# First loop of a two-layer kernel: the causal mask moves from TensorE's score matmuls to an affine select by GpSimd on the exponentials

## The chip, the core and the metric

The kernel runs on one core of a Trainium2 chip. A core has a matmul engine (TensorE, "PE" in the rows, with its weight loads as "PEld"), VectorE ("DVE"), ScalarE ("ACT"), GpSimd ("POOL") and SyncE ("SP", which issues most DMAs here). Each engine works through its own list of instructions in order; they meet through semaphores only. The metric is the device time of one execution in microseconds (us); lower is better.

## The reference, cut to what matters

There are two layers on a batch of 8 sequences of 512 tokens with 128 features. Layer 0 adds an attention block and a mixture-of-experts block to its input; layer 1 adds a gated delta-rule block and a second mixture of experts. The change touches layer 0's attention only (16 heads of 8 features, rotary positions, keys and values from a normalised latent of 32):

```python
scores = jnp.einsum('bhqd,bhkd->bhqk', q, k) / jnp.sqrt(jnp.float32(HEAD_DIM))
causal = jnp.tril(jnp.ones((t, t), dtype=bool))
scores = jnp.where(causal[None, None], scores, -jnp.inf)
attn = jax.nn.softmax(scores, axis=-1)
out = jnp.einsum('bhqk,bhkd->bhqd', attn, v)
```

## The kernel before, in words

The program has two loops of 8 iterations, one iteration per sequence: the first computes layer 0, the second layer 1. Only the first is touched. Its order of work is a list, `schedule_l0` (line 95), which every engine walks; each engine does its own part of a step and skips the rest. An iteration has two halves.

- In the first half TensorE computes the experts' products (`gu`, `wbd`) and, between them, plain scores of which VectorE takes each query's maximum (`max`). The maxima are negated, split in three bf16 parts and put as three extra rows under the queries in `QS`; `KS` has ones there. So a later score matmul gives score minus maximum directly.
- In the second half come four groups g = 0 to 3 of 12 steps `exp`. One group covers two pairs of heads. A head's causal scores against 512 queries are kept transposed (keys on partitions): key tile 0 has 512 query columns, tile 1 has 384, tile 2 has 256, tile 3 has 128. TensorE (`score`, line 616) writes tile 0 in one PSUM bank per head, tiles 1 and 3 together in a second, tile 2 in a third; ScalarE (`expo`, line 1038) turns each bank into exponentials in the SBUF buffer `PT` (20 slots of 512, 10 for even groups and 10 for odd ones). Four banks are used in turn (`SBANK`), so a score must wait until the exponential four steps before has been read.
- After group g comes `pv(g-1)` (line 639): 16 fp32 matmuls that multiply the exponentials by the values, in TensorE's four column groups at once. They end in bank 6, which VectorE copies to `OS` (line 1466); the next `pv` needs that bank. After group 3 stand `pv(2)`, `pv(3)`, the sums and quotient (`nd`, lines 653 to 661 and 1471), and the output projection (line 666).
- Between the `exp` steps of groups 0 to 2 stands the front of the next sequence: layer norm (`fnorm`), transposes (`fT`), the query product (`fq`), latent (`flat`, `flatT`), keys (`fk`), values (`fv`), routing weights (`froute` on VectorE, `fw` on TensorE). It is a chain that goes back and forth between TensorE, VectorE, ScalarE and, for two powers of -0.5, GpSimd (`powers`, line 1215).

The causal mask of the diagonal block (the first 128 columns of each key tile) is added by TensorE: behind the score matmuls a matmul of the bf16 identity with `maskt` (a 128x128 triangle of -1e30) accumulates into the same columns (line 635). The exponential of such a score is zero. GpSimd has two small instructions per iteration. A helper `wait_alone` (line 323) puts a wait on a 128x1 addition of its own, the "tick", when the next instruction should not carry it.

## Time and profile before

| | us |
|---|---|
| median of 3 runs | 2765.76 (2764.23 to 2774.04) |
| the profiled execution, its whole time | 2770.14 |
| its span in the trace | 2768.3 |
| TensorE busy | 2453.1 (89%) |
| VectorE busy | 2028.8 (73%) |
| ScalarE busy | 1136.2 (41%) |
| GpSimd busy | 311.6 (11%) |
| the chain of waits: TensorE, VectorE, issue | 56%, 25%, 12% |

Times in the rows are microseconds from the start of the span. In a group of instructions, the number behind the bar is busy time in all, then the mean duration of one in ns; what follows the second bar is the idle time of the engine just before them and who ended it. The ends of matmuls are modelled, so that busy time of TensorE is not work at its peak. The granted clock of TensorE is printed as a share of full speed; it has two levels, 1.2 and 2.4 GHz (0.5 and 1). The first loop's last output of an iteration is written by line 1477, at 192.6 us for the first sequence and 1053.0 us for the last; the second loop follows.

### The profile page before, as it was taken

To read this page: it belongs to the slowest core of one execution; us is meant where nothing else is said; L and a number is where in the kernel's file an instruction comes from. 1 tells how busy PE (TensorE), PEld (TensorE's weight loads), DVE (VectorE), ACT (ScalarE), POOL (GpSimd) and SP (SyncE) were. 2 spreads that over 40 slices of the span, in tenths; PEclk is the share of its full clock that TensorE was granted. 3 is DMA by queue.
4 is the path that set the end of the run, shared out by engine and by line. 5 is a ranking of instruction groups with operands and counts; after the bars stand their busy time and mean duration, and the time that the engine had idled before them with its cause. 6 is when DMAs were issued, how large, how long until landed. Compare 5 with 4: busy or idle time off the path is not lost.

```text
span 2768.3 us, 48745 instructions
## 1 busy us (share of the span) xinstructions
PE 2453.1 (89%) x15408; PEld 1596.9 (58%) x15408; DVE 2028.8 (73%) x6361; ACT 1136.2 (41%) x2066; POOL 311.6 (11%) x236
## 2 busy tenths in 40 slices
PE   2989888898989887899899899899899899899898
PEld 1434344443444444586586586586586586577576
DVE  4857676685867777768777867867867966966976
ACT  0132322313232234446446445445445445544544
POOL 1000000000000001121121110210210211211211
PEclk8988889898988987999999999999899999899999
DMA  5230413212130312201201201101101101211210
GB/s 157 78 93 24 108 37 88 55 62 72 46 103 25 105 43 66 69 5 58 70 4 59 62 9 62 54 17 62 47 25 62 47 25 36 66 32 32 62 39 31
DMA packets 158271, 152.01 MB, mean 55 GB/s; under 512 B 81128, under 2 KB 122672, under 8 KB 157520
## 3 DMA queue, kind: packets, MB, share of 16 engines
q1 hardware_dynamic: 155024, 142.83, 18.0%
q10 hardware_dynamic: 3008, 6.36, 0.6%
q8 instruction: 105, 1.72, 0.3%
q14 instruction: 134, 1.10, 0.1%
HBM read 121.29 MB, written 27.85 MB: 54 GB/s over the span
## 4 chain that ended last, share of the span: by engine, by line
PE 56%; DVE 25%; issue 12%; ACT 3%; DMA 2%; POOL 1%; SPq 1%; DVEq 0%; ACTq 0%; POOLq 0%
PE bank L910 5%; PE bank L922 5%; PE bank L580 4%; PE bank L592 4%; PE bank L583 4%; PE bank L608 3%; PE bank L502 3%; DVE arena L1605 3%; DVE arena L1663 3%; DVE arena L1661 3%; PE bank L648 3%; PE bank L897 2%; PE bank L879 2%; DVE arena L1617 2%; PE bank L870 2%
## 5 line engine op out<-in xcount | busy, mean ns | idle before, releaser
L922 PEld LDWEIGHTS bank<-wring,arena 128*128 128x128 f32 x2048 | 279.9, 202 | 136.4 <-issue 99.0
L1166 ACT ACTIVATE arena<-bank,w_b 128x512 f32<-128x512 f32 x256 | 175.1, 687 | 369.6 <-PE bank L910 369.3
L910 PE MATMUL bank<-arena,wring 128*128 128x512 f32 x512 | 295.0, 662 | 30.9 <-ACT arena L1166 30.9
L922 PE MATMUL bank<-wring,arena 128*128 128x128 f32 x2048 | 284.7, 287 | 22.8 <-DVE arena L1778 15.2
L1605 DVE SCALAR_TENSOR_TENSOR arena<-bank,w_convw,arena 128x511 f32<-128x511 f32 (+2 forms) x384 | 254.9, 737 | 11.6 <-ACT arena L1076 11.6
L1045 ACT ACTIVATE arena<-bank 128x512 f32<-128x512 f32 (+1 forms) x384 | 172.5, 534 | 186.9 <-PE bank L635 185.3
L1449 DVE CUSTOM_DVE_ANT_0 bank<-bank,arena 128x128 f32<-128x128 f32 (+3 forms) x512 | 249.2, 492 | 0.0
L1036 ACT ACTIVATE arena<-bank 128x512 f32<-128x512 f32 x128 | 76.5, 598 | 397.4 <-PE bank L580 397.4
L502 PE MATMUL bank<-w_ident,arena 128*128 128x128 f32 (+2 forms) x652 | 114.9, 303 | 84.5 <-DVE arena L1345 51.9
L592 PE MATMUL bank<-arena 128*128 128x128 f32 x1088 | 157.5, 288 | 2.7 <-DVE arena L1434 2.7
L580 PE MATMUL bank<-arena 128*128 128x512 f32 x256 | 148.7, 664 | 0.0
L592 PEld LDWEIGHTS bank<-arena 128*128 128x128 f32 x1088 | 131.6, 191 | 21.0 <-issue 10.2
L583 PE MATMUL bank<-arena 128*128 128x512 f32 x256 | 135.9, 613 | 8.2 <-ACT arena L1027 8.2
L502 PEld LDWEIGHTS bank<-w_ident,arena 128*128 128x128 f32 (+2 forms) x652 | 76.5, 138 | 114.3 <-issue 50.4
L1263 POOL TENSOR_TENSOR junk<-arena 128x512 f32<-128x512 f32 x64 | 65.3, 1041 | 671.3 <-DVE arena L1737 393.2
L725 PE MATMUL bank<-arena,w_Wqkvz 128*128 128x512 f32 x256 | 135.2, 655 | 0.0
L326 DVE TENSOR_TENSOR tick<-nhalf 128x1 f32<-128x1 f32 x600 | 94.1, 157 | 50.2 <-PE bank L608 43.7
L910 PEld LDWEIGHTS bank<-arena,wring 128*128 128x128 f32 x512 | 85.3, 201 | 76.2 <-ACT arena L1166 50.8
L1249 POOL TENSOR_TENSOR arena<-arena 128x512 f32<-128x512 f32 x64 | 92.3, 1475 | 293.9 <-ACT arena L1095 185.2
L608 PE MATMUL bank<-arena 48*128 48x128 bf16 (+3 forms) x512 | 109.7, 307 | 15.8 <-DVE arena L1460 10.0
L608 PEld LDWEIGHTS bank<-arena 48*128 48x128 bf16 x512 | 36.2, 92 | 147.7 <-issue 71.0
L1217 POOL TENSOR_TENSOR rstd<-var,nhalf 128x4 f32<-128x4 f32 x9 | 9.1, 1009 | 859.1 <-DVE var L1302 859.1
(284 smaller groups left out, 4845.8 us busy)
## 6 DMA issues: line engine op xcount, KB each, us to landing
wring<-in_w_last SPq DMA_DIRECT2D x66, 512.0 KB, 3.3
arena<-scrw SPq DMA_DIRECT2D x260, 128.0 KB, 3.0
arena<-scrg SPq DMA_DIRECT2D x32, 512.0 KB, 5.4
arena<-scrq SPq DMA_DIRECT2D x36, 192.0 KB, 3.8
arena<-scrk SPq DMA_DIRECT2D x36, 192.0 KB, 4.5
scrn<-arena SPq DMA_DIRECT2D x64, 64.0 KB, 1.9
arena<-scrn SPq DMA_DIRECT2D x8, 512.0 KB, 3.7
scrx<-arena SPq DMA_DIRECT2D x8, 512.0 KB, 3.5
```

The costliest lines, as they stand in the source:

```text
L502: return nc.tensor.transpose(dst, src, W["ident"][0:k, 0:k])
L580: mm(bk[:, :], W["gate0"][:, p, :] if p < PR0 else W["sg"][:], xnT, start=True, stop=True).then_inc(*s["p_gate"].up)
L583: mm(bk[:, :], W["up0"][:, p, :] if p < PR0 else W["su"][:], xnT, start=True, stop=True).then_inc(*s["p_up"].up)
L592: last = mm(bank[7][:, t * P:(t + 1) * P], HID[:, p % 2, t * P:(t + 1) * P], W["down0"][:, p, :] if p < PR0 else W["sd"][:], start=(p == 0 ...
L608: mm(bk[:, 0:w], QS[o:o + KROWS, h // 2, qt * P:(qt + 1) * P], KS[o:o + KROWS, h // 2, 0:w], start=True, stop=True, tile_position=(o, 0)). ...
L725: mm(bk[:, :], W["Wqkvz"][:, m * P:(m + 1) * P], zT, start=True, stop=True).then_inc(*s["p_qkv"].up)
L910: mm(bank[HBANK[f]][:, :], wring[:, e % 2, k * P:(k + 1) * P], xn1T, start=True, stop=True).then_inc(*s["p_fh"].up)
L922: last = mm(bank[o][:, t * P:(t + 1) * P], GH[:, f % 2, t * P:(t + 1) * P], wring[:, e % 2, FC * P + k * D:FC * P + (k + 1) * D], start=(f ...
L1045: fn(PT[:, slot, col:col + w], bank[SBANK[n % 4]][:, 0:w], ACT.Exp, scale=float(HD) ** -0.5).then_inc(*s["a_p"].up)
L1166: fn(GH[:, f % 2, :], bank[HBANK[f]][:, :], ACT.Gelu_apprx_tanh, bias=W["b1"][:, f:f + 1]).then_inc(*s["a_gh"].up)
L1449: v.tensor_tensor_reduce(bk[:, 0:w], bk[:, 0:w], W["maskq"][:, S - w:S], 1.0, PAD, ALU.add, ALU.max, mx[:, col:col + 1]).then_inc(*s["v_ma ...
L1605: ins = v.scalar_tensor_tensor(out=cv[:, k:S], in0=bank[2 + m % 4][:, 0:S - k], scalar=W["convw"][:, m, 3 - k:4 - k], in1=cv[:, k:S], op0= ...
```

## The change: what it does

The mask matmuls are gone. A score matmul now starts and stops its own accumulation and counts one semaphore step (8 per pair of heads; it was one per bank, 6 per pair), and the waits on that semaphore are renumbered to match. GpSimd now walks the list too: after every second `exp` step it waits (with a tick) for the two exponentials and sets the part above the diagonal to zero in both heads' slots with one affine select over 2x128 columns; after the second bank (tiles 1 and 3) it does two such selects. The result is counted on a new semaphore `g_msk`, 6 steps per group, and `pv(g)` waits for that where it waited for ScalarE's `a_p`. The two powers are now separate steps of GpSimd's list (`fnorm`, `flat`). `maskt` is in fp32, is still loaded and has no reader.

```diff
@@ score, pv (TensorE)
                             mm(bk[hh][:, col:col + w], KS[o:o + MROWS, pair, kt * P:(kt + 1) * P],
-                               QS[o:o + MROWS, pair, kt * P:S], start=(col == 0), stop=False, tile_position=(o, 0),
-                               skip_group_check=True)
-                    for hh in range(2):
-                        for kt, col in parts:
-                            last = mm(bk[hh][:, col:col + P], W["identb"][:], W["maskt"][:], start=False, stop=True,
-                                      skip_group_check=True)
-                        last.then_inc(*s["p_score"].up)
+                               QS[o:o + MROWS, pair, kt * P:S], start=True, stop=True, tile_position=(o, 0)
+                               ).then_inc(*s["p_score"].up)
 
                 def pv(g):
-                    pe.wait_ge(*s["a_p"].at(b, 12 * g + 12))
+                    pe.wait_ge(*s["g_msk"].at(b, 6 * g + 6))
@@ expo (ScalarE)
-                    act.wait_ge(*s["p_score"].at(b, n + 1))
+                    act.wait_ge(*s["p_score"].at(b, 8 * (n // 6) + (1, 2, 5, 6, 7, 8)[n % 6]))
@@ SyncE
-                        sp_.wait_ge(*s["p_score"].at(b, 6 * NQ))
+                        sp_.wait_ge(*s["p_score"].at(b, 8 * NQ))
...
-                    sp_.wait_ge(*s["p_score"].at(b, 12 * NQ))
+                    sp_.wait_ge(*s["p_score"].at(b, 16 * NQ))
@@ GpSimd
-            def powers(b, k):
+            def fstat(b, k):
                 pool.wait_ge(*s["v_var"].at(b, 1, k))
                 tt(rstd[:, :], var4[:, :], nhalf[:, 0:NT], ALU.pow).then_inc(*s["g_rstd"].up)
+
+            def flat(b, k):
                 pool.wait_ge(*s["v_lvar"].at(b, 1, k))
                 tt(rstd2, var42, nhalf[:, 0:NT], ALU.pow).then_inc(*s["g_lrstd"].up)
 
-            ahead_of_loop(powers)
+            ahead_of_loop(fstat, flat)
             with pool.Fori(0, LOOPS) as b:
-                powers(b, 1)
+                def causal(g, i):
+                    if i % 2 == 0:
+                        return
+                    wait_alone(pool, *s["a_p"].at(b, 12 * g + i + 1))
+                    slot = 10 * (g % 2) + 5 * (i // 6)
+                    if i % 6 == 5:
+                        part = PT[:, slot + 4, :].rearrange("p (r n) -> p r n", r=2)[:, :, 0:P]
+                    else:
+                        part = PT[:, slot + i % 6 - 1:slot + i % 6 + 1, 0:P]
+                    if i % 6 == 3:
+                        last = PT[:, slot + 2:slot + 4, 3 * P:S]
+                        nc.gpsimd.affine_select(last, last, [[0, 2], [1, P]], ALU.is_ge, 0.0, base=0, channel_multiplier=-1)
+                    nc.gpsimd.affine_select(part, part, [[0, 2], [1, P]], ALU.is_ge, 0.0, base=0, channel_multiplier=-1
+                                            ).then_inc(*s["g_msk"].up)
+
+                steps = {"exp": causal, "fnorm": lambda: fstat(b, 1), "flat": lambda: flat(b, 1)}
+                for step in L0:
+                    steps.get(step[0], nothing)(*step[1:])
```

TensorE, second half of group 2 (line 630: scores; 635: mask; 502: the transposes of `fw`; 648: `pv(1)`), the difference:

```order
-L635 MATMUL bank<-arena,w_identb 128x128 x2
 L502 MATMUL bank<-w_ident,arena 32x128 x4
 L567 REGISTER_ALU x2
 L630 MATMUL bank<-arena 128x384 x2
 L630 MATMUL bank<-arena 128x128 x2
-L635 MATMUL bank<-arena,w_identb 128x128 x4
 L567 REGISTER_ALU x2
 L630 MATMUL bank<-arena 128x256 x2
-L635 MATMUL bank<-arena,w_identb 128x128 x2
```

The score matmuls and `fw` keep their order, and nothing stands between a score and the next step any more.

GpSimd, the body of the first loop before:

```order
L1222 ISA
L1217 TENSOR_TENSOR rstd<-var,nhalf 128x4 [waits v_var]
L1219 TENSOR_TENSOR arena<-arena,nhalf 128x4 [waits v_lvar]
L1222 REGISTER_ALU
L1222 COMPARE_AND_BRANCH
```

and the start of the same body after (line 1210 and 1214: the two powers; 326: the tick; 1229 and 1230: the selects; `a_p` counts exponentials):

```order
L1210 TENSOR_TENSOR rstd<-var,nhalf 128x4 [waits v_var]
L325 ISA
L326 TENSOR_TENSOR tick<-nhalf 128x1 [waits a_p]
L1230 ISA
L1230 AFFINE_SELECT arena<-arena 128x2x128
L325 REGISTER_ALU
L326 TENSOR_TENSOR tick<-nhalf 128x1 [waits a_p]
L1229 AFFINE_SELECT arena<-arena 128x2x128
L1230 AFFINE_SELECT arena<-arena 128x2x128
```

Three more ticks and selects of this kind stand ahead of the second power; in all an iteration has 24 ticks and 32 selects on GpSimd.

## Rows read from the trace of the kernel before

**Rows 1.** The page: busy time, share of the span and instructions of each engine.
```profile
PE 2453.1 (89%) x15408; PEld 1596.9 (58%) x15408; DVE 2028.8 (73%) x6361; ACT 1136.2 (41%) x2066; POOL 311.6 (11%) x236
```

**Rows 2.** By stretch: length, PE, PEld, DVE, ACT, POOL, clock, DMA, GB/s.
```profile
316.50:441.30 124.80, 111.46 (x595) 52.74 (x594) 87.77 (x340) 35.99 (x71) 2.02 (x2) 0.88 0.24 65
441.30:562.10 120.80, 107.45 (x595) 51.46 (x594) 87.83 (x341) 35.99 (x71) 2.02 (x2) 0.92 0.24 67
```

**Rows 3.** Groups of instructions by form, in the first loop.
```profile
L635 PE MATMUL bank<-arena,w_identb 128*128 128x128 bf16 x512 | 70.6, 248 | 0.0
```

**Rows 4.** The chain of waits from 536 to 552 us: start, us, what.
```profile
by line: PE bank L648 35.5%; ACT arena L1045 18.6%; PE bank L630 18.1%; PE bank L635 12.8%; issue 9.0%; DVE arena L1466 4.4%; PE bank L502 3.8%; ACTq L1040 0.7%
540.54 0.33 PE bank L635 x4
541.08 0.22 PE bank L635 x2
548.32 0.22 PE bank L635 x2
```

**Rows 5.** Instructions in order of time: start, us, engine, line; in brackets idle before.
```profile
509.11 1.11 PE L502 MATMUL bank<-w_ident,arena 128*128 128x128 f32 x4 [2.15 <-DVE arena L1345]
...
521.89 0.69 DVE L1307 TENSOR_TENSOR arena<-arena 128x512 f32<-128x512 f32 x1
...
530.42 2.07 PE L544 MATMUL bank<-arena 32*128 32x128 f32 x8 [0.37 <-DVE arena L1382]
...
536.83 3.80 ACT L1045 ACTIVATE arena<-bank 128x512 f32<-128x512 f32 x8 [5.98 <-PE bank L635]
...
539.60 0.33 PEld L502 LDWEIGHTS bank<-w_ident,arena 128*32 128x32 f32 x4 [0.21 <-DVE arena L1415]
...
543.52 0.39 PE L630 MATMUL bank<-arena 51*128 51x512 bf16 x2
...
544.19 5.33 ACT L1045 ACTIVATE arena<-bank 128x512 f32<-128x512 f32 x12 [1.76 <-PE bank L635]
...
551.64 2.36 PE L648 MATMUL bank<-arena 128*32 128x512 f32 x32 [0.81 <-DVE arena L1466]
```

**Rows 6.** Busy time by stretch, around the fall of the clock.
```profile
422.80:426.20 3.40, 2.43 (x24) 1.12 (x28) 0.00 (x0) 3.31 (x8) 0.00 (x0) 1.00 0.24 84
426.20:429.60 3.40, 3.40 (x24) 1.08 (x20) 0.00 (x0) 0.83 (x3) 0.00 (x0) 0.50 0.71 158
518.30:535.40 17.10, 15.45 (x68) 6.19 (x70) 12.98 (x53) 6.39 (x15) 1.01 (x1) 0.50 0.23 81
535.40:538.80 3.40, 2.52 (x36) 1.11 (x28) 3.09 (x22) 1.97 (x5) 0.00 (x0) 1.00 1.06 216
545.60:549.00 3.40, 2.47 (x28) 1.04 (x30) 0.00 (x0) 3.31 (x9) 0.00 (x0) 1.00 0.23 71
```

**Rows 7.** TensorE in order of time: `pv(2)` in the third and fourth iteration, masks.
```profile
425.98 4.05 PE L648 MATMUL bank<-arena 128*32 128x512 f32 x32
...
547.18 0.40 PE L635 MATMUL bank<-arena,w_identb 128*128 128x128 bf16 x4
...
548.47 2.36 PE L648 MATMUL bank<-arena 128*32 128x512 f32 x32
```

**Rows 8.** GpSimd's instructions by form, whole span.
```profile
L1263 POOL TENSOR_TENSOR junk<-arena 128x512 f32<-128x512 f32 x64 | 65.3, 1041 | 671.3 <-DVE arena L1737 393.2 <-DVE arena L1734 278.1
L1210 POOL MEMSET arena<- 128x2048 f32 x1 | 1.8, 1807 | 27.1 <-DVE w_Wout L1292 27.1
L326 POOL TENSOR_TENSOR tick<-nhalf 128x1 f32<-128x1 f32 x9 | 1.8, 195 | 175.9 <-ACT arena L1083 175.9
```

**Rows 9.** Second loop, in order of time: four scans alone, four beside GpSimd.
```profile
1090.66 4.55 DVE L1617 TENSOR_TENSOR_SCAN arena<-arena,w_floor 128x512 f32<-128x512 f32 x4
...
1096.31 6.96 DVE L1617 TENSOR_TENSOR_SCAN arena<-arena,w_floor 128x512 f32<-128x512 f32 x4
1096.57 11.53 POOL L1249 TENSOR_TENSOR arena<-arena 128x512 f32<-128x512 f32 x8 [31.31 <-DVE arena L1629]
```

More of the change, by code:

```diff
@@ L46 @@
     "cos": ([P, S], F32), "sin": ([P, S], F32),
-    "ident": ([P, P], F32), "identb": ([P, P], BF16), "maskq": ([P, S], F32), "maskt": ([P, P], BF16),
+    "ident": ([P, P], F32), "identb": ([P, P], BF16), "maskq": ([P, S], F32), "maskt": ([P, P], F32),
     "grank": ([P, 2, NT, G0, G0], F32),
@@ L306, in build @@
             v_link v_tlink v_flink v_var g_rstd v_xn p_xnT a_xnT p_q p_lat v_q v_k v_lat p_latT v_latT p_k p_v a_v
-            v_lvar g_lrstd a_lexp v_lsfc v_w0 p_w0T v_wt v_qs3 v_ks3 d_scrq d_scrk d_q0 d_k0 d_q1 d_k1
+            v_lvar g_msk g_lrstd a_lexp v_lsfc v_w0 p_w0T v_wt v_qs3 v_ks3 d_scrq d_scrk d_q0 d_k0 d_q1 d_k1
             p_gate0 p_up0 p_gate p_up a_sg v_t v_hid p_down p_max v_max v_nm p_mT v_nmt v_nm3 d_scrm d_m d_m2
@@ L1206, in _ @@
             pool.wait_ge(s["setup_v"].sem, 2)
-            def flat(a):
-                return a
             nc.gpsimd.memset(V32, 0.0).then_inc(s["g_init"].sem, 1)
@@ L1887, in constants @@
     c["maskq"] = mq
-    c["maskt"] = np.where(i > j, NEG, 0.0)
+    c["maskt"] = np.where(i > j, 0.0, -PAD)
     g, o = np.arange(G0)[:, None], np.arange(G0)[None, :]
```

## The prediction, as written before the changed kernel ran

> **What bounds the kernel now.** The page's first part comes first [rows 1]: TensorE is busy for 89% of the span, GpSimd for 11%. That says only that GpSimd has room on average; what the change is worth is read in the first loop's second half, where the masks stand. The groups by form give 512 mask matmuls, 64 in each of the 8 iterations [rows 3]. The view in order of time then shows who waits there, and the chain of waits what of the masks lies on it. I read the fourth iteration (441.3 to 562.1 us) in full; the seven full iterations are alike but for the clock, and two of them stand in [rows 2].
>
> The second half has two parts with different limits.
> - From 504 to 532 us (groups 0 and 1) the limit is the next sequence's front, a chain that TensorE and VectorE hand to and fro. Before every step of it TensorE is idle and waits for VectorE: 2.15 us ahead of the transposes, 0.37 us ahead of the value product, with three such waits between [rows 5]. The masks of groups 0 and 1 lie in those waits; half of all masks cost nothing.
> - From 536 to 552 us (groups 2 and 3) it is ScalarE's exponentials, fed by TensorE, and the two `pv` products. There the chain has 12.8% of 16 us on the masks [rows 4], which is 2.05 us of an iteration.
>
> **What the removed masks give, step by step.** Group 2: ScalarE starts at 536.83 [rows 5]; without the pair of masks ahead of it, it would start about 0.25 us sooner, but the transposes of `fw` at 539.60 wait for VectorE [rows 5], so that gain stops there. Behind `fw`, four masks of 0.33 us and two of 0.22 stand on the chain ahead of `pv(1)` [rows 4]: 0.55 us. Group 3: its first score starts at 543.52 and its first exponential 0.67 us later [rows 5]; with no masks between I take 0.27 off. The 12 exponentials then run back to back for 5.33 us [rows 5], as long as before. Ahead of `pv(2)` one pair, 0.22 us [rows 4]. Sum 0.55 + 0.27 + 0.22 = 1.04 us, in 8 iterations 8.3 us. The least is 0 (if another wait steps in), the most the chain's whole 2.05 us, 16.4 us in all.
>
> **What GpSimd now needs.** Per group 6 ticks and 8 selects of 2x128 elements. A tick is 0.195 us [rows 8]. The trace has no select, so I bound it: a memset of 2048 elements takes 1.81 us [rows 8], which at the same rate is 0.1 + 0.23 = 0.33 us for 256; the top end is the contended tensor operation of rows 9, 11.53 us for eight of 512 elements (some started late), 1.44 us each, taken whole for half the elements. I take 0.62 us: the 1.04 us of the uncontended operation on 512 elements, less the tick's 0.195, halved, and the 0.195 back [rows 8]; a select reads and writes what it does, in place. A group then costs 8 x 0.62 + 6 x 0.195 = 6.1 us of GpSimd, against 5.33 us of exponentials. In groups 0 and 1, which last 25 us, that is hidden; the second power of `powers` comes behind the selects of (0, 7) and is not late.
>
> The wait that can hurt is that of `pv(3)` for the last select, and behind it stand the sums, the reciprocal, the output projection and the next iteration. From 538.0 us, when the second exponential of group 2 is done, two groups of 6.1 us end at 550.2, or, bound by the last exponentials (549.5 us, two selects' worth behind), at 551.8. `pv(3)` starts at 551.64 today, held by VectorE's copy [rows 5]. So at 0.62 the select costs at most what the first paragraph gained, at 0.33 nothing. The point from which it decides is 0.75 us: beyond it `pv(3)` starts at 538.0 + 2.3 + 16 selects, later than today.
>
> The Trainium skill, "GPSIMD Engine Reference" (4.1 Engine selection), says that one-input work there is roughly line-rate, against half rate for two inputs; by the page's 1.2 GHz I estimate 0.2 us of work and some 0.2 of start, and the last select would then never be waited for. No row here shows a one-input operation of this kind.
>
> **What GpSimd takes from VectorE.** Four scans of VectorE took 4.55 us alone and 6.96 us beside GpSimd's tensor operations [rows 9], 53% longer. In the front chain the subtraction at 521.89 (line 1307, 0.69 us) and one more of its kind 1.2 us later stand where the selects of (0, 9), (0, 11) and (1, 1) would run, held back until the second power is done at 520.5. 1.4 us at up to 53% is 0.7; with GpSimd's selects over part of it I take 0.4 us per iteration, 3.2 us in all. The ends are 0 and 6 us.
>
> The Trainium skill, the same page (8. Key points), states that GpSimd shares its SBUF interfaces with VectorE and contends with VectorE instructions that have two SBUF inputs; the scans of rows 9 agree, and a subtraction of two SBUF tensors is of that kind.
>
> **What the missing masks do to the clock.** This is the largest term. The granted clock falls to 0.50 in places [rows 6]: in the third iteration TensorE was busy for 2.43 of the 3.4 us from 422.8, the scores, masks and waits of group 3, and the next 3.4 us ran at half clock. There `pv(2)` took 4.05 us instead of the 2.36 us of the fourth iteration [rows 7], where the same stretch of group 3 (545.6 to 549.0, busy 2.47 us) was not followed by a fall [rows 6]. So group 3 already stands at the edge, and it falls in two of eight iterations. Without masks that stretch loses two pairs and one lot of four (0.40 us by its row [rows 7]), some 0.9 us: 1.5 us busy in place of 2.47. The stretch from 535.4 loses as much of its 2.52 [rows 6]. The masks are also the only matmuls there on all 128 rows and columns; the scores use 51 rows. I expect a fall behind both stretches in nearly every iteration: two more stretches of 3.4 us at half clock, less the quarter of one that is there already, plus a quarter for iterations where the early fall (504 to 511 us) comes one step sooner: 6.8 us.
>
> The price comes from the two iterations in [rows 2]: 124.8 us at 0.88 and 120.8 us at 0.92, nothing else differing. The 0.04 of some 123 us are 9.8 us at half clock, for 4.0 us: 0.41 us per us. 6.8 x 0.41 = 2.8 us per iteration, 22 us in all. The last stretch delays `pv(3)` by itself to about 553 us, so that GpSimd's lag at 0.62 disappears behind it and isn't added.
>
> The Trainium skill, "TensorE: Matmul & The Clock Gate" (Part 1), puts it that the default state is throttled and activity releases the throttle. By that rule taking out matmuls from a sparse stretch is no pure gain; the fall behind the sparse stretch of [rows 6] agrees.
>
> **Nothing else.** SyncE's renumbered waits stand for the same scores; ScalarE's name the same matmuls less the masks; `maskt`, now twice as large, is loaded once ahead of the loop beside megabytes of weights. The second loop is the same code. I put these at 0.
>
> **Sum.** -8.3 + 3.2 + 22 = +17 us. On the profiled execution's 2770.1 us that is 2787; the median of the runs shown is 4.4 us lower, and against it the forecast is 2765.8 + 17 = 2783 us, 0.6% slower.
>
> **Rivals.**
> - The clock stays as it is (24%). For it: two sparse stretches of nearly the same busy time ended differently, so busy time alone does not decide. Against it: the removed part is over a third of what TensorE does there. Then -8.3 + 3.2 = -5, 2761 us.
> - GpSimd becomes the bound (20%). A select above 0.8 us makes `pv(3)` wait past 553 us. At 1.04 us (as long as the uncontended operation on 512 elements [rows 8]) a group is 9.5 us, two end at 557.0, 4.0 us later than in the forecast: 32 us more, 2815 us. At 1.44 us they end at 563.4: 10 us per iteration, about 2865 us. For it: a select works out a condition for every element, which no row of GpSimd's shows. Against it: it reads one tensor and not two.
> - Faster, the other side (8%): all 2.05 us of masks on the chain are gained and the clock doesn't move. That needs `fw` not to hold group 2, its wait for VectorE being only 0.21 us [rows 5], and the exponentials to start as soon as scores are there. 16.4 us less: 2749 us. It decides where the busy stretches around `pv(1)` keep the clock up.
> - That the masks are hidden altogether, and nothing moves, is within the first rival's span.
>
> **How the numbers follow.** The forecast has 48%; its own range is 2772 (one stretch of low clock in place of two) to 2797 (0.7 us of contention and three stretches). A measurement of this kernel can't tell less than about 0.5%, 14 us, from no change. Of the forecast's 48, 30 lie beyond 2779.6 and 18 within; the first rival is within but for 2; the second is slower; the third is faster. Faster 10%, within 40%, slower 50%. The range for 8 in 10 reaches down to 2756, which takes in the clock rival, and up to 2815, the GpSimd rival's first price.
>
> **What would show it.** In the trace after: line 635's matmuls gone and `pv(1)` nearer to `fw` by 0.5 us where the clock is full. The granted clock: iterations of the first loop at 0.86 to 0.88 rather than 0.88 to 0.92, with half clock behind group 3 and in `pv(2)` in most of them, `pv(2)` at about 4 us. A select of about 0.6 us, `pv(3)` waiting for VectorE's copy and not for GpSimd. Line 1307's subtractions longer than 0.69 us where selects run beside them. I am wrong if the clock after group 3 stays at 1.00, or if the first `pv(3)` matmul waits for a select by more than 1 us.

## The result: 40 us slower, and what the profile after shows

| | before | after |
|---|---|---|
| median, runs of both on one chip | 2769.9 (4 runs) | 2809.9 (4 runs, 2804.6 to 2816.9) |
| ratio | 1 | 1.014 [1.0119, 1.0161] |
| the profiled execution's span | 2768.3 | 2802.8 |
| mean granted clock | 0.915 | 0.899 |
| last output of the first loop | 1053.6 | 1093.5 |

The forecast was +17 us; the measured change is +40 us between the medians, and 34.5 us between the two profiled executions. In the profiles the first loop's last output came 39.9 us later, and the second loop, which has the same code, was 5.4 us shorter. Between the profiles of this study the second loop took 1709 to 1728 us, with 216 to 263 us of it at half clock; so totals differ by this too, and the first loop is read by itself below.

The first part of the page after, to be held against [rows 1]: the 512 matmuls of the masks are gone, and TensorE is busy for only 25 us less, since others became longer.
```profile
PE 2428.1 (87%) x14896; PEld 1572.4 (56%) x14896; DVE 2036.6 (73%) x6361; ACT 1134.0 (40%) x2066; POOL 457.7 (16%) x684
```

Three iterations of the kernel after, with the columns of [rows 2] (length, PE, PEld, DVE, ACT, POOL, clock, DMA, GB/s). They are 123.7 to 129.5 us long, against 120.8 and 124.8.
```profile
329.10:452.80 123.70, 103.07 (x531) 48.96 (x530) 89.13 (x341) 35.63 (x71) 20.30 (x58) 0.88 0.24 65
452.80:581.90 129.10, 107.73 (x531) 49.52 (x530) 89.32 (x340) 35.63 (x71) 20.12 (x58) 0.84 0.22 63
581.90:711.40 129.50, 108.53 (x531) 50.35 (x530) 89.35 (x341) 35.63 (x71) 20.35 (x58) 0.83 0.23 62
```
The clock's column separates the short one from the long ones, with equal work and nothing else different: the clock was at half for 30.7 us in the first of them and for 44.4 us in the third. 5.8 us of length for 13.7 us of half clock is 0.42 us per us; the prediction had read 0.41 from [rows 2]. (The Trainium skill, "TensorE: Matmul & The Clock Gate", "HAM oscillation", counts a half of the throttled time as lost. Here it is less than that: TensorE stands idle for part of that time, 1.65 of the 17.1 us at half clock in [rows 6].)

TensorE and ScalarE in order of time, groups 2 and 3 of the fourth iteration (452.8 to 581.9 us), the counterparts of [rows 5] and [rows 7].
```profile
554.96 0.61 PE L502 MATMUL bank<-w_ident,arena 128*32 128x128 f32 x4 [1.59 <-DVE arena L1427]
555.50 0.50 PE L630 MATMUL bank<-arena 51*128 51x384 bf16 x6
555.93 4.05 PE L643 MATMUL bank<-arena 128*32 128x512 f32 x32
...
564.44 4.49 PE L643 MATMUL bank<-arena 128*32 128x512 f32 x32
569.74 4.07 PE L643 MATMUL bank<-arena 128*32 128x512 f32 x32 [0.81 <-DVE arena L1478]
```
```profile
560.42 5.16 ACT L1040 ACTIVATE arena<-bank 128x512 f32<-128x512 f32 x12 [2.84 <-PE bank L630]
```
Line 643 is `pv`, line 1040 the exponential. `pv(1)`, `pv(2)` and `pv(3)` take 4.05, 4.49 and 4.07 us, where before `pv(1)` and `pv(3)` took 2.36 us in all seven full iterations and `pv(2)` in six of them. The wait of `fw` for VectorE has grown from 0.21 us [rows 5] to 1.59; over the seven iterations it is 0.4 to 1.6 us. The 12 exponentials of group 3 take 5.16 us instead of 5.33. And `pv(3)` waits 0.81 us for VectorE's copy (line 1478), as before, and never for a select: from that copy's start to `pv(3)` it is 0.75 us in each of the 7 full iterations of either kernel.

The same groups by stretch; the seventh figure is the granted clock.
```profile
552.90:556.30 3.40, 1.73 (x16) 0.77 (x20) 3.08 (x9) 1.95 (x6) 2.13 (x7) 0.98 0.74 112
556.30:563.10 6.80, 4.90 (x43) 1.63 (x36) 0.69 (x1) 3.96 (x11) 2.50 (x10) 0.75 0.28 89
563.10:566.60 3.50, 3.10 (x18) 0.82 (x22) 0.00 (x0) 2.49 (x6) 2.87 (x11) 0.50 0.27 77
```
TensorE is busy for 1.73 us of the 3.4 in which it waits for `fw`'s weights (2.52 us in the corresponding row of [rows 6]), and the clock falls at 556.2. It comes back at 559.6, while `pv(1)` is still running, falls again at 563.0 behind the scores of group 3, and stays at half up to 573.2, through `pv(2)` and into `pv(3)`.

GpSimd's instructions by form, to be held against [rows 8].
```profile
L1230 POOL TENSOR_SCALAR_AFFINE_SELECT arena<-arena 128x256 f32<-128x256 f32 x192 | 85.9, 447 | 0.3
...
L326 POOL TENSOR_TENSOR tick<-nhalf 128x1 f32<-128x1 f32 x201 | 51.5, 256 | 356.5 <-ACT arena L1040 180.8 <-ACT arena L1078 173.9
...
L1229 POOL TENSOR_SCALAR_AFFINE_SELECT arena<-arena 128x256 f32<-128x256 f32 x64 | 26.1, 408 | 0.0
```
A select takes 0.41 to 0.45 us. The prediction took 0.62, between bounds of 0.33 and 1.44. The estimate worked out from the Trainium skill, "GPSIMD Engine Reference" (4.1 Engine selection), 0.2 us of work and some 0.2 of start, was the better one.

### The profile page after: what moved, and what is told of

Same layout as the page of the kernel before. It is cut to its first block, busy times and chain, and to the rows that moved or that the text cites. A ratio compares the mean times of both kernels' runs of the same rounds, so it can differ in the third digit from the quotient of the medians.

```text
span 2802.8 us, 48326 instructions
## 1 busy us (share of the span) xinstructions
PE 2428.1 (87%) x14896; PEld 1572.4 (56%) x14896; DVE 2036.6 (73%) x6361; ACT 1134.0 (40%) x2066; POOL 457.7 (16%) x684
## 4 chain that ended last, share of the span: by engine, by line
issue 36%; PE 35%; DVE 19%; POOL 4%; ACT 2%; DMA 2%; SPq 1%; DVEq 0%; POOLq 0%; ACTq 0%
PE bank L905 5%; PE bank L917 4%; DVE arena L1617 3%; PE bank L502 3%; DVE arena L1675 3%; DVE arena L1673 3%; DVE arena L1629 2%; PE bank L892 2%; PE bank L874 2%; POOL arena L1230 2%; PE bank L865 2%; PE bank L836 2%; PE bank L827 1%; PE bank L855 1%; POOL tick L326 1%
## 5 line engine op out<-in xcount | busy, mean ns | idle before, releaser
L643 PE MATMUL bank<-arena 128*32 128x512 f32 (+3 forms) x1024 | 126.1, 659 | 6.5 <-DVE arena L1478 6.5
```

## The accounts of one iteration, for all kernels

This table is worked out from the profile of each kernel as the mean of the 7 full iterations of the first loop. "Half clock" is the sum of the stretches whose granted clock is 0.5. "Rest" is the length less 0.41 times the half clock, so what the iteration would be at full clock. The next two columns are medians of the kernel and of the kernel before, run beside it. The last is the granted clock over the whole execution, as the mean of all timed runs, with that of the kernel before beside it in brackets; it takes in the second loop, but it doesn't hang on one execution.

| kernel | length | half clock | rest | median | before | clock, all runs |
|---|---|---|---|---|---|---|
| before | 122.9 | 26.3 | 112.1 | | | |
| after | 127.7 | 39.5 | 111.5 | 2809.9 | 2769.9 | 0.901 |
| e1 masks gone | 123.8 | 32.7 | 110.4 | 2776.4 | 2774.2 | 0.909 (0.918) |
| e2 masks kept, selects added | 125.8 | 30.7 | 113.2 | 2801.9 | 2774.2 | 0.910 (0.918) |
| e3 after, short fillers in all groups | 124.8 | 29.3 | 112.8 | 2781.0 | 2774.2 | 0.918 (0.918) |
| e4 after, short fillers in groups 2 and 3 | 124.3 | 28.3 | 112.7 | 2787.2 | 2774.2 | 0.910 (0.918) |
| e5 masks gone, VectorE delayed | 125.0 | 34.6 | 110.8 | 2783.4 | 2770.6 | 0.909 (0.918) |
| e6 before, dense fillers | 121.3 | 8.8 | 117.7 | 2754.9 | 2770.6 | 0.942 (0.918) |
| e7 after, dense fillers | 121.1 | 6.8 | 118.3 | 2755.9 | 2770.6 | 0.944 (0.918) |
| e8 after, again | 127.9 | 40.0 | 111.5 | 2805.3 | 2771.1 | 0.902 (0.921) |
| e9 masks gone, 0.9 us longer | 126.2 | 37.1 | 111.0 | 2795.5 | 2771.1 | 0.905 (0.921) |
| e10 after, 0.9 us longer | 129.9 | 44.9 | 111.5 | 2819.5 | 2771.1 | 0.901 (0.921) |
| e11 before, dense fillers, `fw` later | 118.7 | 5.4 | 116.5 | 2739.3 | 2771.1 | 0.948 (0.921) |
| e12 before, 0.9 us longer | 122.9 | 23.9 | 113.1 | 2779.7 | 2773.1 | 0.918 (0.917) |
| e13 before, VectorE delayed | 124.3 | 28.3 | 112.7 | 2779.2 | 2773.1 | 0.916 (0.917) |

How far to trust a row: eight times the difference in length to before agrees with the difference of the medians within some 8 us (e3: 15 against 7; e10: 56 against 48; e12: 0 against 7; e1: 7 against 2; e2: 23 against 28; e13: 11 against 6). A profile is one execution, and 8 us of time are 2.5 us of half clock per iteration, so the half clock is not better than that. Some profiles are of a run at the edge of its kernel's: e1's is the fastest of ten, e4's the slowest of ten.

Three things are read from it.
- The rest adds up: masks gone -1.7 us, selects +1.1, both -0.6, whichever is done first.
- The half clock grows with either: masks gone +6.4 us, selects +4.4, both +13.2. That both is more than the sum isn't shown: the 2.4 us between them are within what one profile can tell. By the last column half clock in a whole execution (twice what is missing from 1, times the span) grows by 53 us in e1, by 47 in e2 and by some 100 in the kernel after, which is the sum. By the times, both cost 14 us more than e1 and e2 together (0.014 against 0.0011 + 0.008, with 11 us either way), and by e8's ratio for the kernel after 7 us more (16 either way).
- The selects by themselves, with every mask in place, lose more time than the missing masks by themselves: 22 us against 3 by the ratios.

## The experiments

The first theory was that of the prediction, now for the whole 40 us: TensorE has less to do in stretches that were sparse already, the clock falls, and the `pv` products run at half. The rivals were the selects (GpSimd held up by them, or VectorE beside them), and that the half clock only follows from a longer iteration.

**e1: the masks alone taken out.** The masks' matmuls are removed as in the change, with `p_score` renumbered; there are no selects, and `pv` waits for `a_p` as before. It leaves the causal mask of the diagonal blocks out.
```diff
-                        for kt, col in parts:
-                            last = mm(bk[hh][:, col:col + P], W["identb"][:], W["maskt"][:], start=False, stop=True,
...
                 def pv(g):
                     pe.wait_ge(*s["a_p"].at(b, 12 * g + 12))
```


> The kernel before with TensorE's mask matmuls taken out and nothing in their place (the causal mask is left out). TensorE's list is that of the changed kernel, GpSimd's that of before. If the loss comes from the clock that falls where the masks are missing, this kernel has nearly all of it: 2800 to 2806 us, half clock for 40 us or so of an iteration of the first loop, as in the changed kernel (41 to 44), and the 5 us below it are VectorE's part. If GpSimd's selects, their waits or their contention made the loss, this kernel only gains the masks' 1.0 us per iteration: 2762 us, clock as before (20 to 31 us of half clock per iteration).

Measured: 2776.4 against 2774.2 us, ratio 1.0011 [0.9994, 1.0028]. Three of its iterations:
```profile
192.90:317.60 124.70, 104.95 (x531) 49.02 (x530) 87.87 (x341) 35.69 (x71) 2.01 (x2) 0.86 0.24 65
...
563.60:690.80 127.20, 107.72 (x531) 49.42 (x530) 87.86 (x341) 35.69 (x71) 2.02 (x2) 0.84 0.24 64
690.80:813.90 123.10, 103.22 (x531) 48.94 (x530) 87.83 (x340) 35.52 (x71) 2.01 (x2) 0.88 0.24 66
```
The half clock grows by 6.4 us per iteration, close to the 6.8 of the prediction, and mostly where it was forecast: there is a fall of the clock behind group 2 in all seven iterations and behind group 3 in four, where the kernel before has none and one. At full clock the removal gives 1.7 us per iteration: between the 1.04 taken and the 2.05 us that the chain of waits had [rows 4]. The two nearly cancel: the removal by itself costs 2 us by the medians and 7 by the profile, where the prediction's two terms for it gave 14.

**e2: the selects alone added.** The kernel after with the masks' matmuls still in the scores (the two places against the kernel before).
```diff
+                    pe.wait_ge(*s["g_msk"].at(b, 6 * g + 6))
...
                             last = mm(bk[hh][:, col:col + P], W["identb"][:], W["maskt"][:], start=False, stop=True,
```


> The changed kernel with the mask matmuls back on TensorE, as before, and GpSimd's ticks, selects and pv's wait for them kept (the mask is applied twice). If the clock made the loss: before plus what the selects take from VectorE on the chain, about 0.9 us per iteration by the two traces (0.5 in the split of q, 0.4 in the routing), 2777 us, half clock 20 to 31 us per iteration. If GpSimd made the loss: 2810 us or a little more, at whatever clock.

Measured: 2801.9 us, ratio 1.008 [1.0053, 1.0108]. So most of the loss comes with the selects even where every mask is still there. VectorE, on its way to `fw`, is later in three places: from the latent's normalisation to the scaling of its transposes it is 3.66 us instead of 3.13, the split of the keys into bf16 parts, just ahead of the routing, takes 2.78 us instead of 2.36, and the routing 7.04 us instead of 6.81; 1.2 us in all. Two stretches of e2, the second half of group 2 with `fw` in it and what follows:
```profile
546.90:550.40 3.50, 2.47 (x30) 1.04 (x22) 3.16 (x23) 2.44 (x6) 0.88 (x4) 0.98 1.06 203
550.40:557.30 6.90, 6.82 (x44) 2.45 (x46) 1.70 (x3) 2.91 (x7) 3.15 (x11) 0.51 0.33 80
```
TensorE's row of `pv(1)` there is
```profile
553.57 4.17 PE L648 MATMUL bank<-arena 128*32 128x512 f32 x32
```
A fall behind group 2, which no full iteration of the kernel before has and five of e2's seven have, though TensorE was busy for 2.47 us as in the stretches of [rows 6]. A longer wait for VectorE doesn't explain this one: in this iteration TensorE goes on from the scores to `fw` with less than 0.1 us between, as before.

**e3 and e4: fillers in place of the masks.** The kernel after, and behind each score as many 128x128 matmuls of the identity as there were masks, into a bank that is free; in e3 in all groups, in e4 in groups 2 and 3 alone.
```diff
+                        spare = bank[6] if g < 2 or (g == 2 and i >= 8) else bank[4]
+                        for _ in range(2 * len(parts)):
+                            mm(spare[:, 0:P], W["identb"][:], W["identb"][:], start=True, stop=True)
```


> The changed kernel with a filler in place of each mask matmul: identity times identity, 128x128 in bf16, into a PSUM bank that nobody reads then, behind the score's semaphore, so that ScalarE never waits for it. Clock theory: the missing matmuls matter as activity alone, whatever they compute, so the clock comes back; 7 us for contention, 3 us less for exponentials that start sooner: 2774 us. GpSimd theory: 2810 us. If what matters is only that exponentials start sooner (ScalarE finishing early and TensorE idle for it), it stays near 2810 too, since they still do.

> The same fillers in groups 2 and 3 only. Clock theory: the falls behind groups 2 and 3 go (13.7 us of half clock in two of three iterations), the longer early one, in groups 0 and 1 (27 us against 24 before in the mean), stays: 2778 to 2785 us. If the early falls cost as much as the late ones, 2790 us or more. GpSimd theory: 2810 us.

Measured: 2781.0 us, 1.0024 [1.0004, 1.0044], and 2787.2 us, 1.005 [1.0032, 1.0069], where the kernel after has 1.014. Work that computes nothing takes back 32 us in one kernel and 25 in the other (0.0116 and 0.009 of 2770 us); the half clock falls from 39.5 to 29.3 and 28.3 us per iteration, and the fillers' own cost is the 1.2 to 1.3 us by which the rest grows. Over all ten runs e3 has the clock of the kernel before, 0.918, and e4 0.910: the half clock of e4 in the table is the first loop's alone, and in that profile the second loop has 30 us more half clock than before's. The fillers do not stand on the chain of the exponentials as the masks did (nothing reads their bank), so e3 is not e2 under another name: it has the selects and as many matmuls as e2, and is 21 us faster. Why was not looked at.

**e5: VectorE's delay without the selects.** e1 with two VectorE additions on spare data, 352 columns ahead of the scaling of the latent's transposes and 128 in the routing. It leaves the causal mask of the diagonal blocks out, as e1 does.
```diff
+                v.tensor_tensor(spend, spend, spend, ALU.add)
                 dve.wait_ge(*s["p_latT"].at(b, 1, k))
...
                 link(v.tensor_scalar(rank, rank, 2.0, None, ALU.is_lt))
+                v.tensor_tensor(junk[:, 4, :], junk[:, 4, :], junk[:, 4, :], ALU.add)
```


> The kernel of the first experiment (masks gone, GpSimd as before, causal mask left out) with two operations more on VectorE that nobody needs: 352 columns ahead of the latent's scaling (0.53 us, what the selects added there) and 128 columns in the routing (0.29 us, what they added there). First theory, GpSimd's share is only that it slows VectorE, and the delay leaves TensorE idle for longer ahead of the transposes of fw and of the latent, so that the clock falls more often: most of the changed kernel's loss comes back, 2795 to 2810 us, 12 us of half clock per iteration behind the front in place of 6.8. Second theory, the selects harm in another way (their waits, ScalarE, SBUF): only the delays themselves, 8 x 0.8 us: 2783 us.

Measured: 2783.4 us, ratio 1.0041 [1.0019, 1.0063]; 3.57 us for the latent's part and 7.01 us for the routing, 0.64 us more than without the additions. That is about half of what the selects do: the third place, the split of the keys, was overlooked, and takes 2.36 us here as before. That this delay turns e1 into the kernel after had asked for 2795 to 2810 us, and is refuted: it gives 8 us more than e1 by the ratios, and the kernel after 36 more. Five of its iterations are alike, 126.3 us with 37.5 us of half clock; the first two have 23.9 and 30.7. None has 44.4 us as the kernel after has. Over all ten runs the clock is e1's, 0.909.

**e6 and e7: activity held up by force.** Denser fillers (512 columns each) where TensorE waits, the same in the kernel before and the one after, but for four in place of one ahead of `fw` and e3's short ones in e7.
```diff
+                    for _ in range({(0, 2): 8, (0, 4): 1, (0, 8): 3, (1, 2): 4, (1, 6): 7, (1, 10): 3, (2, 2): 1, (2, 6): 1,
+                                    (3, 2): 1, (3, 4): 1, (3, 6): 1, (3, 8): 1}.get((g, i), 0)):
+                        mm(spare[:, :].rearrange("p (a b) -> p a b", a=4), W["identb"][:],
+                           W["identb"][:].unsqueeze(1).broadcast_to((P, 4, P)), start=True, stop=True)
```


> The kernel before with fillers of 512 columns (identity times identity, into a bank that nobody reads then) where TensorE waits for VectorE: 26 in groups 0 and 1, 2 in group 2, 4 in group 3; results unchanged. If idle stretches are what lets the clock fall, half clock goes from 26 us to 10 or less per iteration and 16 x 0.41 us x 8 = 52 us go: 2720 us. If the front's speed hangs on VectorE's chain alone, TensorE's clock buys nothing there and the fillers stand in the way: 2775 us or more.

> The changed kernel with the same long fillers (three more ahead of fw, where it idles longer) and one short filler for each mask. If the clock is the cause of the whole loss, the changed kernel loses it here: half clock as in the kernel before with these fillers, and the two kernels differ only by 0.8 us of VectorE per iteration against 1.0 to 1.9 us of masks: 0 to 9 us faster than it, about 2715 us. If the selects cost something beside the clock, it stays 20 us or more above that kernel.

Measured: 2754.9 us, 0.9944 [0.9925, 0.9964], and 2755.9 us, 0.9948 [0.9929, 0.9966]. An iteration of each, e6 first:
```profile
312.00:432.00 120.00, 108.95 (x627) 52.44 (x626) 87.82 (x340) 35.89 (x72) 2.01 (x2) 0.97 0.25 67
```
```profile
312.80:434.90 122.10, 110.08 (x630) 52.64 (x629) 89.15 (x340) 35.62 (x71) 20.32 (x58) 0.97 0.24 66
```
With the clock at 0.97 in both, the change costs 1 us, with 8 either way: 32 selects and 24 ticks on GpSimd (20.32 us of work per iteration), 1.3 us more of VectorE. The fillers of the two are not quite the same, and both kernels wait for VectorE ahead of `fw`; but with the table's column of rest (111.5 us after, 112.1 before) and with e3 this puts the loss in the clock. I had expected 2720 us for e6, and it is 35 us more. The rest grows by 5.6 us per iteration: the fillers take time of their own, and TensorE waits for the routing ahead of `fw`, which in e11 below gives back some 15 us:
```profile
528.96 1.04 PE L502 MATMUL bank<-w_ident,arena 128*32 128x128 f32 x4 [2.19 <-DVE arena L1424]
```
With the front 4 us shorter at full clock (23.2 us from the first score to the value product's end, instead of 27.3), TensorE comes to `fw` that much earlier than VectorE is done.

**e8, e9 and e10: the iteration's length.** e8 is the kernel after again. In e9 (e1) and e10 (after), four dense matmuls of some 0.2 us each stand in the iteration's first half, far from the groups. e9 leaves the causal mask of the diagonal blocks out.
```diff
+                    if p == 3:
+                        for _ in range(4):
+                            mm(bank[6][:, :].rearrange("p (a b) -> p a b", a=4), W["identb"][:],
+                               W["identb"][:].unsqueeze(1).broadcast_to((P, 4, P)), start=True, stop=True)
```


> The changed kernel itself, timed beside the other runs of this call. If its 40 us are its own: 2805 to 2817 us, ratio 1.014 again, an iteration of the first loop 129.1 to 129.5 us in two of three. If they were a matter of that chip or hour: nearer to 2783, the time of masks gone plus VectorE's delay.

> The kernel of the first experiment (masks gone, GpSimd as before, causal mask left out) with 4 dense matmuls of 512 columns more in the first half of an iteration, where TensorE is full: each iteration is some 0.9 us longer, and nothing of the second half is touched. First theory: what the missing masks cost depends on how the iterations fall on the clock's changes, and masks gone alone was a lucky case; then the time moves by much more than the 7 us that were added, towards 2800 us, with pv at 4.5 us in most iterations. Second theory: without the selects the clock holds whatever the length: 2784 us.

> The changed kernel with the same 4 dense matmuls more in the first half. First theory (the pattern of the clock hangs on the iteration's length, and the changed kernel has hit a bad one): not 2817 us but another value between 2780 and 2830, and another pattern than 129.5, 123.7, 129.1 us. Second theory (the selects themselves keep TensorE at half clock): 2817 us, the same falls in the same places.

Measured: e8 2805.3 us, 1.0117 [1.007, 1.0163], with the same sequence of long and short iterations, 129.5, 123.7 and 129.1 us, its first full one apart (131.0). e9 2795.5 us, 1.0077 [1.0046, 1.0107]: 19 us over e1, where the added work is worth 7. e10 2819.5 us, 1.0163 [1.0112, 1.0214]: in place of the sequence, six of the seven full iterations are alike, 129.7 us (the first 131.2), and the short one never comes. Two iterations of e9, the second as long as the kernel after's longest, with no select in it:
```profile
196.90:319.40 122.50, 102.55 (x535) 48.79 (x534) 87.83 (x341) 35.63 (x71) 2.02 (x2) 0.89 0.24 66
319.40:448.90 129.50, 109.97 (x535) 50.10 (x534) 87.80 (x341) 35.69 (x71) 2.01 (x2) 0.83 0.23 62
```
By the ratios it is 18 us, with 10 either way. So the small cost of e1 was partly luck. Without masks an iteration can be 122.5 or 129.5 us long with the same work in it, and after a shift of 0.9 us far from the change the long ones were more frequent: six of e9's seven are 125.3 us or longer, and one of e1's.

**e12 and e13: the two controls with the masks in place.** e12 is the kernel before with e9's four matmuls, e13 the kernel before with e5's two additions; neither has other edits.

> The kernel before, masks and all, with the same four dense matmuls (128 rows, 512 columns, some 0.9 us) in each iteration's first half that moved the kernel without masks from 2776 to 2795 us. First theory: that jump came of the missing masks, which leave the second half open to wherever the clock's changes fall, while the masks' activity holds it: 7 us of added work, 2777 us (to 2780), pv(1) to pv(3) at 2.4 us in nearly all iterations, half clock about 26 us per iteration. Second theory: any of these kernels loses some 20 us when its iteration is lengthened so, and the jump says nothing on masks: 2790 us, half clock 30 us per iteration or more.

> The kernel before, masks kept, with the two VectorE operations on spare data (352 columns in the latent's part of the chain, 128 in the routing's) that stood in for the selects' contention on the kernel without masks; no selects. First theory: what selects cost beside kept masks (2802 us) is VectorE's delay on the chain and the half clock that follows from TensorE's longer waits: 2792 to 2802 us, exponentials of group 2 to those of group 3 9.0 us where it was 7.4, pv(1) at 3 us or more. Second theory: the selects slow the second half otherwise too (their reads and writes of the buffer, their load on every engine there), and the delay alone costs its own 0.8 us per iteration: 2776 to 2780 us.

Measured: e12 2779.7 us, 1.0025 [1.0007, 1.0042], so the added work and nothing more. Two of its iterations:
```profile
316.80:439.70 122.90, 109.07 (x599) 52.32 (x598) 87.84 (x341) 35.83 (x71) 2.01 (x2) 0.90 0.24 66
...
931.20:1053.90 122.70, 108.29 (x597) 52.14 (x596) 87.81 (x340) 33.95 (x69) 2.01 (x2) 0.90 0.25 66
```
All seven are between 122.7 and 122.9 us, with 23.9 us of half clock; a sparse stretch before `pv(2)` is still followed by a fall. `pv(1)` and `pv(3)` take 2.4 us in each; `pv(2)` takes 3.0, the one point where the expectation was too good. The theory that any kernel loses 20 us by such a shift is refuted: with the masks in place this one costs its own length. The masks' absence is worth 6.4 us of half clock (e1 against before), 13.2 (e9 against e12), 6.3 (e5 against e13) or 8.8 (after against e2).

e13: 2779.2 us, 1.0031 [1.0013, 1.0049]. The delay is there (3.57 and 7.02 us), and it costs 6 us where the selects, beside the same masks, cost 28 (9 and 22 by the ratios). Three of its iterations:
```profile
318.00:444.30 126.30, 112.81 (x595) 52.68 (x594) 88.41 (x343) 35.93 (x71) 2.01 (x2) 0.86 0.23 64
444.30:567.70 123.40, 109.95 (x595) 52.01 (x594) 88.37 (x342) 35.94 (x72) 2.01 (x2) 0.89 0.23 65
567.70:693.40 125.70, 111.81 (x594) 53.22 (x594) 88.34 (x342) 35.97 (x71) 2.01 (x2) 0.88 0.24 64
```
By the medians the second theory was right, that the delay costs little more than its own length, 0.6 us per iteration. The profiled execution, 5 us above the median, has three iterations of seven near e2's length of 126 us, and four short ones where e2 has one. What the selects add besides the delay of these two places was not found, but the stand-in was too small: it leaves out the split of the keys, where the casts and subtractions of VectorE are longer with selects beside them. The second cast, before and after:
```profile
531.58 0.43 DVE L1308 CAST arena<-arena 128x512 bf16<-128x512 f32 x1
```
```profile
546.33 0.65 DVE L1320 CAST arena<-arena 128x512 bf16<-128x512 f32 x1
```
So it is not excluded that VectorE's delay, in its full size, is what the selects do. Neither that nor e1 with selects on spare data, which would keep all of their contention and none of `pv`'s waits, was tried.

**e11: a version that beats both.** e6 with `fw` moved behind step (3, 2), two more fillers in group 2, and the spare bank's waits adapted.
```diff
-             (1, 10): [("fv",)], (1, 11): [("froute",)], (2, 6): [("fw",)]}
+             (1, 10): [("fv",)], (1, 11): [("froute",)], (3, 2): [("fw",)]}
```


> The kernel before with the long fillers of the sixth experiment, and fw moved from step (2, 6) to (3, 2): with the fillers TensorE stood 5 us in group 2 waiting for VectorE's routing weights. If that wait is what ate the fillers' gain, it goes: 4.6 us of the 12.0 between the first exponentials of groups 2 and 3, 8 x 4.6 = 37 us, 2718 us. If the wait only moves to group 3 or to the weights' way back through DRAM (hid waits for d_wb): 2750 us.

Measured: 2739.3 us against 2771.1, 0.9888 [0.9852, 0.9925]: 31 us faster than the kernel before and 66 us faster than the one after (e8, run beside it). `fw` waits for nothing any more, and an iteration has the clock at 0.99:
```profile
526.55 0.60 PE L502 MATMUL bank<-w_ident,arena 128*32 128x128 f32 x4
```
```profile
307.60:426.20 118.60, 108.10 (x629) 52.23 (x628) 87.82 (x341) 35.65 (x71) 2.02 (x2) 0.99 0.24 68
```
I had expected 2718 us. The iteration is 118.7 us; the rest column has 116.5 for it, 4.4 us above before's: the fillers take time, and TensorE still waits for VectorE (1.2 us ahead of `pv(1)`). How it divides was not measured.

## Why the prediction was off

**The step that failed** is what GpSimd's selects cost, the term "What GpSimd takes from VectorE": I took 0.4 us per iteration, 3.2 us in all, with ends of 0 and 6 us, and put their effect on TensorE's clock at nothing, without a reason. Measured with all masks kept (e2), the selects cost 28 us between the medians, 22 by the ratio; beside missing masks (after against e1) 36 us by the ratios. Per iteration that is 1.1 us at full clock, and 4.4 us (e2) to 6.8 us (after against e1) more at half clock.

The clock's term was counted for the missing masks alone, and as such it had the right size: 6.8 us taken, 6.4 measured in e1. The places were right, and the price of 0.41 per us held. But e9, with the same masks missing and the iteration 0.9 us longer, has 37.1 us of half clock where e12 has 23.9: that 6.8 came so near to the measured 6.4 is in part luck. The sum with the measured figures is
- masks' removal at full clock: -1.7 us per iteration, -14 us in all (the prediction: -8.3);
- selects at full clock: +1.1 us, +9 (the prediction: +3.2);
- half clock by the missing masks: 6.4 x 0.41 = 2.6 us, +21 (the prediction: +22);
- half clock by the selects beside missing masks: 6.8 x 0.41 = 2.8 us, +22 (the prediction: nothing);
- sum +38 us, against 39.9 us in the first loop of the profile and 40 us between the medians.

The half clock by the selects is what the forecast lacks. That it is there is shown by e2; how selects on GpSimd bring TensorE's clock down is not shown. My explanation was that they delay VectorE, so that TensorE waits longer and the clock falls behind its waits. For it: TensorE's wait ahead of `fw` grew from 0.21 us to 0.4 to 1.6. Against it: e5 and e13, which delay VectorE by about half as much, cost 8 and 9 us by the ratios, of which 5 are the delay's own length; and e2's fall behind group 2 comes in iterations without such a wait too. Nor is it shown that masks stop such a fall once it has begun: in one iteration of e13, with masks, `pv(3)` takes 4.2 us.

**Term by term.**
- Masks on the chain: 1.04 taken, 1.7 measured (e1), inside its bounds of 0 and 2.05. With no masks ahead of them the exponentials of group 3 also became shorter, 5.16 for 5.33 us, which I had left equal.
- Select: 0.62 taken, 0.41 to 0.45 measured. The rival that GpSimd is the bound was far off: its point was 0.75 us (0.71 by the prediction's own figures, 551.64 less 540.3 over 16 selects).
- Contention: 0.4 us per iteration taken, 0.75 at most; the front of the kernel after shows 0.53 us (latent), 0.53 us (the split of the keys, which the prediction passed over) and 0.30 us (routing), 1.4 us in all. Two rows of the kernel after, the subtractions of line 1319 and 1321 (1307 and 1309 before, 0.69 us [rows 5]), with selects beside them:
```profile
535.80 0.78 DVE L1319 TENSOR_TENSOR arena<-arena 128x512 f32<-128x512 f32 x1
...
537.30 0.91 DVE L1321 TENSOR_TENSOR arena<-arena 128x512 bf16<-128x512 f32 x1
```
  It goes both ways: a select beside the second of them took twice its usual time.
```profile
537.62 0.85 POOL L1230 TENSOR_SCALAR_AFFINE_SELECT arena<-arena 128x256 f32<-128x256 f32 x1
```
  The Trainium skill, "GPSIMD Engine Reference" (8. Key points), names contention with VectorE's instructions of two SBUF inputs, and the trace agrees: 13% to 32% here, 53% for the scans of [rows 9]. The casts to bf16, with one input, are longer too, 0.65 us instead of 0.43.
- The granted clock by iteration was to be 0.86 to 0.88 and is 0.83 to 0.88; `pv(2)` was to take about 4 us and takes 4.5 in five of seven iterations; `pv(3)` waits for VectorE's copy, as forecast.
- The rival that the clock stays (2761 us) and the faster one (2749 us) are refuted by those rows; that the change costs nearly nothing where the clock stays up can be seen in e7.
- The range, 2756 to 2815, held the time; the forecast's own range, 2772 to 2797, did not. Its upper end allowed for one stretch of 3.4 us more than the forecast, where there were nearly two.

**What stays open.** How the selects lower the clock. Of the 6.8 us of half clock that the kernel after has beyond e1, e5's delay of VectorE gives about 2 by its profile and none by the clock of all its runs, and a mere shift in length gives 4.4 (e9); they are not separate in the kernel after. What selects do beside kept masks more than the delay of e13 (22 us between the medians of e2 and e13, 14 between their ratios) was not isolated: the rest of VectorE's delay, 0.5 to 0.7 us per iteration, is one candidate that no run tested. Whether missing masks and selects together cost more than the sum is open as well.

## What to carry to other kernels

Work on an engine that is the bound by its busy share may be what keeps its clock up: before removing it, look at the granted clock on both sides of the place, and price the half clock that follows, not only the instructions. Price the clock for each part of a change, also for work that is moved to an engine with room: here the 32 selects on GpSimd, for which no matmul of TensorE was held up, cost more than the missing matmuls. And try a part by itself before taking its cost for settled: a shift of 0.9 us elsewhere changed what the missing masks cost. And where the clock is at half for a fifth of a loop, idle waits filled with matmuls that compute nothing are worth a trial: here they gave 0.6%, and 1.1% once the wait that they laid bare was moved.

## What the runs showed of the hardware that I had not expected

- The same work added can cost different times. Four dense matmuls in the first half (0.9 us per iteration) moved the kernel without masks by +19 us, the kernel before by +7 us, and the kernel after by 14 us, with nearly all iterations alike at 129.7 us.
- Repeating a loop with no change can have a stable sequence of iterations: 129.5, 123.7, 129.1 us in two separate profiles of the kernel after, 126.3 us five times in e5, 122.9 us seven times in e12.
- A GpSimd affine select of 128x2x128 fp32 elements takes 0.41 us alone, up to 0.85 beside a VectorE operation that reads two SBUF tensors. VectorE's cast of 128x512 elements from fp32 to bf16 takes 0.43 us alone and up to 0.65 beside selects, its subtraction 0.69 us and up to 0.91.
- A second loop with unchanged code took 1709 to 1728 us between the profiles, with 216 to 263 us of half clock in it.
